# The order of phase one and of the first step of a graph attention layer, and two adjacency loads moved ahead of the first gathers

## The chip, the cores and the metric

The kernel runs on one core of a Trainium2 chip, all in fp32. The time is that of one execution on the device, in microseconds; lower is better. Engines are named as in the profile: PE is TensorE (PEld its weight loads), DVE VectorE, ACT ScalarE, POOL GpSimd, SP SyncE. SP, ACT and POOL also issue transfers; every transfer of the core runs on the same 16 DMA engines.

## The reference, cut to what matters

One graph attention layer over 4096 nodes with 256 features and 8 heads of 32. The adjacency is a 4096 x 4096 int32 matrix with few ones, dense in the first rows.

```python
mask = adj + eye(n)
q, k, v = (h @ Wq.T + bq), (h @ Wk.T + bk), (h @ Wv.T + bv)     # each as (n, 8, 32)
scores = einsum('nhd,mhd->hnm', q, k) / sqrt(32)
scores = where(mask == 0, -1e9, scores)
ctx = einsum('hnm,mhd->nhd', softmax(scores), v).reshape(n, 256)
h1 = layer_norm(h + ctx @ Wo.T + bo)
ff = relu(h1 @ W1.T + b1) @ W2.T + b2
out = layer_norm(h1 + ff)
```

## The kernel before

Rows are worked on in 32 tiles of 128. The kernel never builds the score matrix. It searches each row of the adjacency for its ones (`find_dve`, a search instruction on DVE of 4.43 us for 4104 columns), gathers the keys and values of the neighbours found from a table in memory, and scores those alone.

Phase one fills the tables. PE projects keys and values of two tiles at a time, 16 pairs, in `project_kv(i)`; each pair is 16 matmul instructions. ACT copies a pair from PSUM (`take_kv`), POOL adds the key bias (`bias_k`), and the rows go to `kv_table` in memory (`store_kv` on ACT for the last two pairs, groups of four tiles on POOL before that). Pairs of query tiles go the same way: `project_q` on PE, `take_q` on ACT, `store_q` on POOL, into `q_table`. Of the 16 query pairs, `Q_BEFORE` are projected ahead of the steps and the others in gaps of steps 0 and 1, listed by `q_pairs(step, gap)`; pair 0 is projected in the middle of phase one. `take_q(i)` waits until the store of pair i-4 has landed, since there are four staging buffers. Meanwhile DVE searches the first adjacencies, tile 0 (`TILE0`, the dense rows, in 14 pieces) among them.

A chunk of four transposed input tiles (`xT_all[c]`) serves two pairs. SP issues the chunks and the adjacencies on one queue: two halves of chunk 0, adjacency 0, chunks 1 and 2, adjacency 1, chunk 3, the adjacency of tile 0, chunks 4 to 7, adjacencies 2 and 3, weights. Adjacency s goes into buffer s % 2, once adjacency s-2 has been searched (`load_adj`).

Then come the steps `STEPS`, two tiles each at first (b0, b1_, b2, ...). For each step: `load_own` on SP loads the tiles' own rows; POOL issues gathers of 128 rows, two aligned ones (`gather_aligned`), two edge ones (`gather_edges`) and two of queries (`gather_queries`); DVE multiplies and sums the edge scores (`edge_scores_dve`) and the own scores (`own_scores_dve`); PE spreads the edge scores over rows (`ell_pe`), and prepares the next step's lists (`starts_pe`, ACT's `distance_act`, DVE's `rt_dve`, `lists_pe`, `cols_dve`, then the gathers); DVE takes the maximum, ACT the exponential, DVE the sums; DVE searches the first adjacency of the step after next; PE hands the maxima to the edges (`tr_pe`); DVE weights the values and searches the second adjacency; PE sums the values (`sum_pe`). From step 2 on, the dense work of a group of four tiles (output projection `post_pe_attn`, feed-forward `post_pe_ff`, `post_pe_out`) fills the gaps in PE's order. The program of each engine is in order, so the place of a call in these lists is its priority. The work of tile 0 is spread over later steps.

The lines of SP ahead of the steps are

```python
            load_own(sp, STEPS[0])
            sp.wait_ge(got_edges[STEPS[0].par], 2 * STEPS[0].U * 16)
            load_adj(sp, 4)
            load_adj(sp, 5)
```

and `tables_ready(eng, q)` (lines 976 to 985) is what a gather or an own load waits for: all stores of keys and values, and the store of the step's own query pair.

Of the kernel before, what the change touches and what calls it, by code (L numbers as in the profile page):

```python
# [5 lines left out]
ALU = mybir.AluOpType  # L6
# [128 lines left out]
def build(nc, xT, adj, wqkvT, bq, bk, bqkv, woT, w1T, w2T, cols, g2, be2, out):  # L135
    with ExitStack() as ctx:
# [88 lines left out]

        bias_q_cols = scores0[:, 0:D].rearrange("p (k n) -> p k n", k=KC)
# [53 lines left out]
        s_const = sem("s_const")  # L280

# [81 lines left out]
        def job(g, first_tile, at, bank, signals):  # L363
# [31 lines left out]
        (s_gw, s_gx, s_gkt_ps, s_gkt, s_gadj, s_gmask, s_gdiag, s_gxq, s_gqt_ps, s_gqt, s_gscores, s_gmasked, s_gmax, s_gnm,  # L395
         s_gprobs, s_gpt_ps, s_gpt, s_gpv, s_grl, s_gctx, s_gv, s_gctxT_ps, s_gctxT) = [sem(n) for n in (
            "s_gw s_gx s_gkt_ps s_gkt s_gadj s_gmask s_gdiag s_gxq s_gqt_ps s_gqt s_gscores s_gmasked s_gmax s_gnm "
            "s_gprobs s_gpt_ps s_gpt s_gpv s_grl s_gctx s_gv s_gctxT_ps s_gctxT").split()]

        CONSTS = 25  # L400
        WEIGHT_DMAS = 5
# [396 lines left out]
        def lists_pe(pe, q):  # L798
            pe.wait_ge(rt_ready, q.p + 1)
            pe.wait_ge(distance, 2 * q.p + 2)  # L800
# [186 lines left out]
        def gather_aligned(pool, q):  # L987
# [6 lines left out]
            tables_ready(pool, q)  # L994
# [11 lines left out]
        def gather_edges(pool, q, us=None):  # L1006
            pool.wait_ge(cols_ready, q.p + 1)
            tables_ready(pool, q)
# [6 lines left out]
        def gather_queries(pool, q):  # L1015
            pool.wait_ge(row_ready, q.b + 1)
            for u in range(q.U):
# [4 lines left out]
        def load_own(sp, q):  # L1022
            tables_ready(sp, q)
# [291 lines left out]
        def general_dve(dve):  # L1315
            with dve.Fori(0, TILES) as t:
# [5 lines left out]
                for h in range(HEADS):  # L1322
                    n = t * HEADS + h
                    dve.wait_ge(s_gscores, n + 1)
                    nc.vector.tensor_tensor(gS, flat(ps[:]), gmask, ALU.add).then_inc(s_gmasked, 1)
                    dve.wait_ge(s_gmasked, n + 1)
                    nc.vector.tensor_reduce(gstat[:, 0:1], gS, AX_X, ALU.max).then_inc(s_gmax, 1)
                    dve.wait_ge(s_gmax, n + 1)
# [75 lines left out]
        def _(sp):  # L1404
# [68 lines left out]
        def _(pool):  # L1473
# [59 lines left out]
            for q in STEPS:  # L1533
# [53 lines left out]
        def _(act):  # L1587
# [29 lines left out]
            for i in range(PAIRS):  # L1617
                take_kv(i)
# [335 lines left out]
```

## Time and profile before

| what | value |
|---|---|
| time, median of 3 runs | 555.47 us (554.21 to 555.52) |
| span of the profiled execution | 554.5 us, from its first to its last instruction; no time of its own beside the span is given for it |
| PE busy | 483.4 us, 87% of the span |
| DVE busy | 425.2 us, 77% |
| POOL busy | 262.3 us, 47% |
| ACT busy | 214.5 us, 39% |
| moved by DMA | 140.94 MB, 254 GB/s on average |
| mean granted TensorE clock | 0.937 |

Shares of busy time are averages over stages with different limits. Phase one ends near 70 us, step 0 begins on DVE at 86.6 us, step 1 at 108.5 us, step 2 at 127.8 us, and the feed-forward work begins at 148.5 us. In the rows below, the first number is the start and the second the duration, in us; in square brackets stands how long the engine sat idle before the row, and what it was released by.

### The profile page before, as it was taken

How to read it: one execution, taken by the hardware profiler on the slowest of the kernel's cores; microseconds unless marked ns; L12 is line 12 of the kernel's file. 1: busy time of each engine (PE TensorE's matmuls, PEld its weight loads, DVE VectorE, ACT ScalarE, POOL GpSimd, SP SyncE). 2: the span in 40 equal slices, each digit the busy share in tenths (PEclk: the TensorE clock that was granted, in tenths of full speed). 3: DMA queues.
4: the chain of work that ended last, by engine and by line, in shares of the span. 5: the costliest groups of instructions: out<-in, count | busy, mean ns of one | idle time of the engine just before them, and what ended most of it. 6: DMA issues, size and time to landing. Idle time of an engine off the chain costs nothing.

```text
span 554.5 us, 7282 instructions
## 1 busy us (share of the span) xinstructions
PE 483.4 (87%) x2274; PEld 376.7 (68%) x2274; DVE 425.2 (77%) x978; ACT 214.5 (39%) x526; POOL 262.3 (47%) x381
## 2 busy tenths in 40 slices
PE   5999999757699899799989989979878888789994
PEld 4888888655458757675875776668435767458883
DVE  0648696998979999999999987869988898550103
ACT  1244343324362463345336255423443143532430
POOL 6444347363633556745754553515625555305133
PEclk9999989999699999989989999978788799799998
DMA  7999868999999798998898785344765842401011
GB/s 278 418 417 418 318 214 330 400 409 420 398 329 351 266 366 261 366 348 287 323 348 318 247 292 187 138 165 148 262 222 163 302 143 58 134 1 39 0 39 42
DMA packets 39771, 140.94 MB, mean 254 GB/s; under 512 B 4904, under 2 KB 16552, under 8 KB 35632
## 3 DMA queue, kind: packets, MB, share of 16 engines
q1 hardware_dynamic: 24608, 95.03, 45.3%
q0 software_dynamic: 13328, 43.55, 22.7%
q10 hardware_dynamic: 1792, 1.85, 1.0%
q8 instruction: 20, 0.33, 0.2%
q14 instruction: 23, 0.19, 0.1%
HBM read 123.61 MB, written 16.80 MB: 253 GB/s over the span
## 4 chain that ended last, share of the span: by engine, by line
PE 51%; DVE 19%; DMA 10%; issue 8%; ACT 6%; POOL 5%; SPq 0%; POOLq 0%; ACTq 0%; DVEq 0%
PE ps L1086 15%; PE ps L1099 12%; PE ps L1719 10%; DVE found L504 6%; DMA xT_all<-in_xT 4%; PE ps L843 2%; PE ps L1066 2%; DMA work<-q_table,row_of 2%; POOL slots L1011 2%; DMA adj_buf<-in_adj 2%; PE ps L846 1%; ACT xT_all L1143 1%; PE ps L1076 1%; DMA early<-in_wqkvT 1%; PE ps L1054 1%
## 5 line engine op out<-in xcount | busy, mean ns | idle before, releaser
L504 DVE FIND_INDEX8 found<-ones,adj_buf 128x8 uint32<-128x4105 int32 (+5 forms) x40 | 138.7, 3467 | 0.0
L1086 PE MATMUL ps<-xT_all,w 128*128 128x512 f32 (+1 forms) x288 | 125.7, 585 | 0.3 <-ACT xT_all L1116 0.2
L1099 PE MATMUL ps<-w,xT_all 128*128 128x256 f32 x512 | 122.7, 395 | 2.9 <-ACT xT_all L1133 1.6
L1099 PEld LDWEIGHTS ps<-w,xT_all 128*128 128x128 f32 x512 | 99.2, 199 | 17.7 <-ACT xT_all L1133 2.7
L1086 PEld LDWEIGHTS ps<-xT_all,w 128*128 128x128 f32 x288 | 56.0, 203 | 47.6 <-issue 44.1
L1011 POOL DMA_INDIRECT slots<-kv_table,col_of x54 | 55.9, 1035 | 48.3 <-DVE col_of L587 36.4
L1133 ACT ACTIVATE xT_all<-ps,col_table 128x512 f32<-128x512 f32 (+1 forms) x72 | 45.8, 642 | 57.1 <-PE ps L1086 52.3
L1719 PE MATMUL ps<-early,xT_all 128*128 128x256 f32 x256 | 60.2, 398 | 6.1 <-DMA early<-in_wqkvT 6.1
L1719 PEld LDWEIGHTS ps<-early,xT_all 128*128 128x128 f32 x256 | 50.7, 200 | 14.2 <-DMA xT_all<-in_xT 4.7
L1153 DVE BATCH_NORM_STATS2 stats<-ps 128x6 f32<-128x256 f32 x62 | 22.1, 418 | 36.5 <-PE ps L1054 36.5
L954 ACT ACTIVATE xT_all<-ps,col_table 128x256 f32<-128x256 f32 (+1 forms) x38 | 14.5, 432 | 84.5 <-PE ps L846 84.5
L1003 POOL DMA_INDIRECT slots<-kv_table,found x32 | 33.9, 1060 | 27.8 <-PE ps L846 10.7
L1018 POOL DMA_INDIRECT work<-q_table,row_of x40 | 39.7, 992 | 11.1 <-issue 11.0
L1192 POOL TENSOR_TENSOR rstd<-mv,eps_col 128x4 f32<-128x4 f32 (+1 forms) x17 | 6.0, 355 | 76.8 <-DVE mv L1159 76.4
L843 PE MATMUL ps<-work,slots 128*128 128x128 f32 x160 | 29.2, 293 | 13.6 <-DVE slots L708 12.8
L1066 PE MATMUL ps<-wo,xT_all 128*128 128x256 f32 x128 | 35.9, 405 | 3.7 <-issue 2.5
L1735 PE MATMUL ps<-early,xT_all 128*128 128x256 f32 x128 | 36.4, 410 | 1.0 <-ACT slots L1601 1.0
L1517 POOL TENSOR_TENSOR slots<-slots,early 128x512 f32<-128x512 f32 x16 | 20.2, 1265 | 33.7 <-ACT slots L1601 33.7
L843 PEld LDWEIGHTS ps<-work,slots 128*128 128x128 f32 x160 | 24.4, 203 | 16.5 <-DVE slots L708 15.0
L1601 ACT COPY slots<-ps 128x1024 f32<-128x1024 f32 x16 | 16.2, 1013 | 41.6 <-PE ps L1719 41.6
L1003 POOL DMA_INDIRECT slots<-kv_table,aligned_idx x16 | 16.6, 1040 | 27.9 <-PE ps L846 19.9
L1201 POOL TENSOR_TENSOR early<-early,row_g 128x1024 f32<-128x1024 f32 (+1 forms) x8 | 17.8, 2227 | 25.0 <-DVE slots L708 10.4
(180 smaller groups left out, 821.7 us busy)
## 6 DMA issues: line engine op xcount, KB each, us to landing
adj_buf<-in_adj SPq DMA_DIRECT2D x31, 2048.0 KB
xT_all<-in_xT SPq DMA_DIRECT2D x14, 512.0 KB, 24.5
kv_table<-slots POOLq DMA_DIRECT2D x7, 1024.0 KB, 11.2
slots<-kv_table SPq DMA_DIRECT2D x12, 512.0 KB
q_table<-slots POOLq DMA_DIRECT2D x16, 256.0 KB
out_dram<-early SPq DMA_DIRECT2D x7, 512.0 KB
q_own<-q_table SPq DMA_DIRECT2D x12, 256.0 KB
slots<-in_adj SPq DMA_DIRECT2D x1, 2048.0 KB, 23.0
```

The lines of the kernel that those rows point to most:

```text
L504: last = nc.vector.max_index(dst, ones8[:], part)
L843: nc.tensor.matmul(to, edge_slots(q)[:, c, feats], onehot[q.par][:, c, :], start=(u == 0), stop=False)
L1003: nc.gpsimd.indirect_dma_start(to, None, kv_dram, bass.IndirectOffsetOnAxis(ap=idx, axis=0)).then_inc(got_aligned[q.par], 16)
L1011: nc.gpsimd.indirect_dma_start(edge_slots(q)[:, u, :], None, kv_dram, bass.IndirectOffsetOnAxis(ap=col_of[q.par][:, u:u + 1], axis=0)).the ...
L1018: nc.gpsimd.indirect_dma_start(q_edge[q.par][:, u, :], None, q_dram[q.no // 2], bass.IndirectOffsetOnAxis(ap=row_of[q.par][:, u:u + 1], ax ...
L1066: nc.tensor.matmul(to, q["ctxT"][:, k, j * P:(j + 1) * P], wo[:, k, :], start=(k == 0), stop=False)
L1086: last = nc.tensor.matmul(ps[:, q["bank"] + f % 2, 0:q["g"] * P], w1[:, k, f * P:(f + 1) * P], q["h1T"][:, k, :], start=(k == 0), stop=(k ...
L1099: nc.tensor.matmul(to, q["ffT"][:, f, j * P:(j + 1) * P], w2[:, f, :], start=(f == 0), stop=False)
L1133: nc.scalar.activation(q["ffT"][:, f, :], ps[:, q["bank"] + f % 2, 0:q["g"] * P], ACT.Relu, bias=bias_1[:, f:f + 1]).then_inc(q["ff"], 1)
L1153: last = nc.vector.bn_stats(q["stats"][k][:, j, :], tile_out(q, q["bank"] + 2 * k, j))
L1719: last = nc.tensor.matmul(ps[:, kv_bank(i, part), j * D:(j + 1) * D], xT_all[:, c, k, r * P:(r + 1) * P], wqkv[:, k, (1 + part) * D:(2 + p ...
L1735: nc.tensor.matmul(to, xT_all[:, c, k, r * P:(r + 1) * P], wqkv[:, k, 0:D], start=(k == 0), stop=False)
```

## The change

The change reorders phase one and the first step and touches no arithmetic.

- PE runs two matmuls on a constant tile (`warm`, 512 columns of ones that DVE writes first) before its first data. The first pair is projected by `first_kv`: keys of both tiles, then values of both tiles, where it was keys and values of one tile and then of the other.
- Query pair 0 is projected behind the last key and value pair. `Q_BEFORE` falls from 6 to 4, and pairs 4 and 5 move to gap 1 of step 0, pair 6 from gap 0 to gap 2, with their copies and stores.
- ACT stores pair 14 ahead of copying pair 15, and pair 15 at once; then it takes query pair 0; then tile 0's distances, then those of step 1 (which were in step 0).
- DVE searches adjacency 2 before it waits for tile 0's starts, and searches piece 12 of tile 0 before `rt_dve(b0)`. Tile 0's `rt_dve` comes after both searches of step 1's adjacencies. Tile 0's `cols_dve` and `onehot0_dve` move from ahead of step 0 to inside it, behind the edge scores. In step 0 the own scores come before the edge scores.
- Gathers of keys wait for the key tables alone, and only the gathers of queries and the own loads wait for the query tables.
- SP loads adjacency 4 ahead of the own rows of step 0 and adjacency 5 behind them, each when its buffer is free.
- A semaphore is saved in the fallback path, which these inputs do not take.

```diff
-        Q_BEFORE = 6
+        Q_BEFORE = 4
         def q_pairs(i, gap):
             if i == 0:
-                return ((6,), (), (7, 8), (9, 10), (11,), ())[gap]
+                return ((), (4, 5), (6, 7, 8), (9, 10), (11,), ())[gap]
...
-        def tables_ready(eng, q):
+        def keys_ready(eng):
             for i in range(STAGES):
                 eng.wait_ge(s_kv_out[i], (GROUPS // STAGES if i < STAGES - 1 else GROUPS // STAGES - 1) * 16)
-                if q.first:
-                    eng.wait_ge(s_q_out[i], PAIRS // STAGES * 16)
-            eng.wait_ge(s_kv_last, 2 * 16)
+            eng.wait_ge(s_kv_last, 2 * 16)
+
+        def queries_ready(eng, q):
+            if q.first:
+                for i in range(STAGES):
+                    eng.wait_ge(s_q_out[i], PAIRS // STAGES * 16)
             pair = (q.no + q.T - 1) // 2
             eng.wait_ge(s_q_out[pair % STAGES], (pair // STAGES + 1) * 16)
...
+            load_adj(sp, 4)
             load_own(sp, STEPS[0])
-            sp.wait_ge(got_edges[STEPS[0].par], 2 * STEPS[0].U * 16)
-            load_adj(sp, 4)
             load_adj(sp, 5)
...
+                for p in q_pairs(i, 1):
+                    store_q(p)
                 if soon:
                     gather_edges(pool, soon)
...
             for i in range(PAIRS):
+                if i == PAIRS - 1:
+                    store_kv(PAIRS - 2)
                 take_kv(i)
...
-                if i == 13:
-                    take_q(0)
+            store_kv(PAIRS - 1)
+            take_q(0)
             distance_act(act, TILE0)
-            store_kv(PAIRS - 2)
-            store_kv(PAIRS - 1)
             mask_act(act, TILE0)
+            distance_act(act, STEPS[1])
             for i in range(1, Q_BEFORE):
                 take_q(i)
...
-                if i + 1 < NB:
+                if 0 < i < NB - 1:
                     distance_act(act, STEPS[i + 1])
...
+            pe.wait_ge(warm_ready, 1)
+            for _ in range(WARM):
+                nc.tensor.matmul(ps[:, ELL, :], warm[:, 0:P], warm, start=True, stop=True)
+            first_kv()
+            for i in range(1, PAIRS):
                 project_kv(i)
...
-                if i == 13:
-                    project_q(0)
             starts_pe(pe, TILE0)
-            for i in range(1, 4):
-                project_q(i)
-            lists_pe(pe, TILE0)
-            for i in range(4, Q_BEFORE):
+            for i in range(Q_BEFORE):
                 project_q(i)
             starts_pe(pe, b1_)
+            lists_pe(pe, TILE0)
...
+            for us in ((13,), (12,)):
+                find_dve(dve, TILE0, 0, us)
+            rt_dve(dve, b0)
...
+            find_dve(dve, b1_, 0)
             starts0_dve(dve)
-            find_dve(dve, b1_, 0)
-            rt_dve(dve, TILE0)
             find_dve(dve, b1_, 1)
-            cols_dve(dve, TILE0)
-            onehot0_dve(dve)
             listed_dve(dve, b1_)
             spill_dve(dve, b1_)
+            rt_dve(dve, TILE0)
             for q in STEPS:
...
-                edge_scores_dve(dve, q)
-                own_scores_dve(dve, q)
+                if i == 0:
+                    own_scores_dve(dve, q)
+                    edge_scores_dve(dve, q)
+                    cols_dve(dve, TILE0)
+                    onehot0_dve(dve)
+                else:
+                    edge_scores_dve(dve, q)
+                    own_scores_dve(dve, q)
```

## Rows read from the trace of the kernel before

**Rows 1.** Busy us (and instructions) of each engine, granted clock, DMA share, GB/s, by stretch

```profile
70.00:80.00 10.00, 9.80 (x62) 8.69 (x60) 9.57 (x17) 5.62 (x18) 3.94 (x5) 0.94 0.65 219
...
90.00:100.00 10.00, 9.26 (x57) 8.04 (x56) 6.90 (x16) 3.79 (x10) 7.75 (x9) 1.00 0.99 416
...
150.00:175.00 25.00, 24.57 (x99) 16.09 (x98) 21.39 (x40) 10.40 (x26) 8.84 (x8) 0.99 0.94 340
```

**Rows 2.** The chain that ended last, two of its pieces: start us, us, what

```profile
70.85 5.22 DMA q_table<-slots
...
109.50 20.59 DMA xT_all<-in_xT
```

**Rows 3.** Timeline of POOL: first gather, two stores of queries

```profile
77.04 1.06 POOL L1003 DMA_INDIRECT slots<-kv_table,found  x1 [5.45 <-DMA q_table<-slots]
...
91.96 0.77 POOL L1508 DMA_DIRECT2D q_table<-slots  x1
...
97.74 1.54 POOL L1508 DMA_DIRECT2D q_table<-slots  x2
```

**Rows 4.** Timeline of DVE, 37 to 136 us

```profile
37.01 0.48 DVE L566 TENSOR_SCALAR work<-work,spill 128x128 f32<-128x128 f32 x2 [4.47 <-ACT idx_all L907]
...
68.66 0.17 DVE L559 SCALAR_TENSOR_TENSOR mids<-ps,spill 128x14 f32<-128x14 f32 x1 [3.57 <-PE ps L796]
...
80.84 0.16 DVE L575 TENSOR_SCALAR row_of<-ps 128x14 uint32<-128x14 f32 x1
...
82.05 2.88 DVE L594 TENSOR_SCALAR work<-row_mid,ps 128x128 f32<-128x128 f32 x14
...
86.58 0.69 DVE L603 TENSOR_TENSOR work<-work,slots 128x512 f32<-128x512 f32 x1 [1.09 <-DMA work<-q_table,row_of]
...
88.22 1.22 DVE L618 TENSOR_TENSOR slots<-slots,q_own 128x1024 f32<-128x1024 f32 x1
...
96.23 0.09 DVE L504 MATCH_VALUE_LOAD found<-ones,adj_buf 128x8 int32 x1 [2.90 <-DMA adj_buf<-in_adj]
...
108.50 0.68 DVE L603 TENSOR_TENSOR work<-work,slots 128x512 f32<-128x512 f32 x1
...
135.47 0.16 DVE L578 TENSOR_SCALAR row_at<-ps 128x2 f32<-128x2 f32 x1 [1.52 <-PE ps L805]
```

**Rows 5.** Busy PE and PEld, granted clock, DMA share, GB/s: key and value matmuls alone

```profile
13.00:14.00 1.00, 1.00 (x4) 0.80 (x3) 1.00 0.93 327
14.00:15.00 1.00, 1.00 (x7) 0.87 (x6) 1.00 1.09 362
```

**Rows 6.** Timeline of PE, 59 to 83 us

```profile
59.26 1.03 PE L1735 MATMUL ps<-early,xT_all 128*128 128x256 f32 x4
...
61.43 7.07 PE L1719 MATMUL ps<-early,xT_all 128*128 128x256 f32 x32
...
76.57 4.13 PE L805 MATMUL ps<-first_idx,work 128*128 128x18 f32 x28 [0.20 <-DVE work L566]
80.54 2.05 PE L1735 MATMUL ps<-early,xT_all 128*128 128x256 f32 x4
```

**Rows 7.** Load of input chunk 1 (issue at 2.8 us), with time to landing

```profile
L1407 SPq DMA_DIRECT2D xT_all<-in_xT x1: 1267/1267/1267, 2.8 to 2.8; - x1
...
DMA to landing us min/median/max: 13.4/13.4/13.4
```

**Rows 8.** Timeline of ACT

```profile
17.35 1.01 ACT L1601 COPY slots<-ps 128x1024 f32<-128x1024 f32 x1 [2.67 <-PE ps L1719]
...
68.54 1.01 ACT L1601 COPY slots<-ps 128x1024 f32<-128x1024 f32 x1 [2.44 <-PE ps L1719]
...
104.97 0.59 ACT L1607 COPY slots<-ps 128x512 f32<-128x512 f32 x1 [3.43 <-DMA q_table<-slots]
```

**Rows 9.** Stores of the last two key pairs by ACT: time to landing

```profile
DMA to landing us min/median/max: 2.9/3.4/3.9
```

**Rows 10.** Busy PE, granted clock, DMA share, GB/s after tile 0's lists

```profile
83.00:86.00 3.00, 3.00 (x11) 0.56 0.54 186
```

More of the change, by code:

```diff
@@ L799, in lists_pe @@
             pe.wait_ge(rt_ready, q.p + 1)
-            pe.wait_ge(distance, 2 * q.p + 2)
+            pe.wait_ge(distance, 2 * (STEPS[1].p if q.first else q.p) + 2)
             wait(pe, cols_ready, q.p)
@@ L1022, in load_own @@
         def load_own(sp, q):
-            tables_ready(sp, q)
+            keys_ready(sp)
+            queries_ready(sp, q)
             wait(sp, acc_ps, q.before)
@@ L1710, in project_kv @@
                     c, r = (2 * i + j) // GROUP, (2 * i + j) % GROUP
-                    if i == 0 and j == 0:
-                        pe.wait_ge(s_first_xT, 16)
                     if r == (2 if c == 0 else 0):
@@ L1715, in project_kv @@
                     for part in range(2):
-                        if i == 0 and j == 0:
-                            pe.wait_ge(s_wqkv[1 + part], 16)
                         for k in range(KC):
@@ L1720, in project_kv, with first_kv @@
                                                     wqkv[:, k, (1 + part) * D:(2 + part) * D], start=(k == 0), stop=(k == KC - 1))
+                last.then_inc(s_kv_ps, 1)
+            def first_kv():
+                order = [(j, part) for part in range(2) for j in range(2)]
+                for j, part in order:
+                    if (j, part) == (0, 0):
+                        pe.wait_ge(s_first_xT, 16)
+                    if j == 0:
+                        pe.wait_ge(s_wqkv[1 + part], 16)
+                    for k in range(KC):
+                        last = nc.tensor.matmul(ps[:, kv_bank(0, part), j * D:(j + 1) * D], xT_all[:, 0, k, j * P:(j + 1) * P],
+                                                wqkv[:, k, (1 + part) * D:(2 + part) * D], start=(k == 0), stop=(k == KC - 1))
                 last.then_inc(s_kv_ps, 1)
@@ L1741, in _ @@
             b0, b1_ = STEPS[0], STEPS[1]
-            for i in range(PAIRS):
+            pe.wait_ge(warm_ready, 1)
[3 more added lines that the diff above has]
+            for i in range(1, PAIRS):
                 project_kv(i)
@@ L1828, in _ @@
             b0, b1_ = STEPS[0], STEPS[1]
-            pieces0 = ((13,), (12,), (11,), (10,), (9,), (8, 7), (6, 5), (4, 3), (2, 1, 0))
-            for i in range(PAIRS):
-                if i == 1:
-                    dve.wait_ge(s_const, CONSTS)
-                    find_dve(dve, b0, 0)
-                if i == 3:
-                    find_dve(dve, b0, 1)
-                    listed_dve(dve, b0)
-                    spill_dve(dve, b0)
-                if i == 6:
-                    rt_dve(dve, b0)
-                if 5 <= i <= 13 and pieces0[i - 5]:
-                    find_dve(dve, TILE0, 0, pieces0[i - 5])
-                if i == 10:
-                    cols_dve(dve, b0)
-                if i == 13:
-                    listed_dve(dve, TILE0)
-                    spill_dve(dve, TILE0)
+            nc.vector.memset(warm, 1.0).then_inc(warm_ready, 1)
+            dve.wait_ge(s_const, CONSTS)
+            find_dve(dve, b0, 0)
+            find_dve(dve, b0, 1)
+            listed_dve(dve, b0)
+            spill_dve(dve, b0)
+            for us in ((13,), (12,)):
+                find_dve(dve, TILE0, 0, us)
+            rt_dve(dve, b0)
+            for us in ((11,), (10,), (9,), (8,)):
+                find_dve(dve, TILE0, 0, us)
+            cols_dve(dve, b0)
+            for us in ((7, 6), (5, 4), (3, 2), (1, 0)):
+                find_dve(dve, TILE0, 0, us)
+            listed_dve(dve, TILE0)
+            spill_dve(dve, TILE0)
+            find_dve(dve, b1_, 0)
             starts0_dve(dve)
-            find_dve(dve, b1_, 0)
-            rt_dve(dve, TILE0)
             find_dve(dve, b1_, 1)
-            cols_dve(dve, TILE0)
-            onehot0_dve(dve)
             listed_dve(dve, b1_)
             spill_dve(dve, b1_)
+            rt_dve(dve, TILE0)
             for q in STEPS:
```

18 lines of the change are left out of this document (11 added, 7 removed).

## Prediction

> **What bounds the kernel now.** I read the windows by stage first, then the chain of waits up to 150 us, then the timelines of DVE, PE, ACT and POOL. From 150 us on PE is busy 24.57 of 25 us [rows 1]: the dense work runs without a gap, so what the change can win is the time until that work starts, and all of it is then handed on to the end. Ahead of it there are three stages. Until 68.5 us the key and value matmuls follow one another. From there to 86.6 us nothing heavy is the limit: the chain goes through a store of queries of 5.22 us [rows 2], the first gather at 77.04 us [rows 3], and the landing of the last gather, for which DVE starts step 0 at 86.58 us [rows 4]. From 86.58 us DVE sets the pace: step 0 lasts until 108.50 us [rows 4], 21.92 us, with one large hole, 2.90 us of waiting for adjacency 4, which was held back behind the gathers; 19.0 us of it are work. The DMA engines are 0.65 busy from 70 to 80 us and 0.99 from 90 to 100 us [rows 1], so work moved from the second stretch to the first takes free capacity.
>
> I make the sum on the start of step 0's edge scores (86.58), the start of step 1 (108.50) and the start of dense work.
>
> **Phase one.** The first four matmul instructions wait for their weights twice, because keys and values of one tile come first. The new order has eight instructions of work with the first weights. Four instructions touch the us from 13 to 14, and seven the us after it [rows 5]: there the clock went from its low level, 1.2 GHz, to the high one, 2.4 GHz. At the high one an instruction takes 7.07/32 = 0.22 us [rows 6], so 0.43 at the low one. The warming matmuls and the new order would together finish chunk 0, 32 instructions, some 3 us earlier, were the clock high from 9 us on. But chunk 1 is issued at 2.8 us and lands 13.4 us later, at 16.2 us [rows 7], and PE finished pair 1 just before 17.35 us, when ACT copied it [rows 8]. So only about 17.2 - 16.2 = 1.0 us can be taken; with eight instructions done at 8.2 us, 24 more fit before 16.2 us even if the clock stayed low until 13.9 us. I price the warming at next to nothing and both edits at 1.0 us. Bounds: 0 if chunk 1 lands later, 1.1.
>
> Pair 0 of the queries leaves phase one: two tiles of 1.03 us and two small transposes each, from 59.26 to 61.43 us, 2.17 us [rows 6]. The copy of pair 15, at 68.54 us [rows 8], then starts at 68.54 - 1.0 - 2.2 = 65.4 us.
>
> **To the first gathers.** The bias of pair 15 is ready 2.4 us after that, 67.75 us, and ACT stores it; the last two such stores landed in 2.9 and 3.9 us [rows 9]. Keys are ready at 71.6 us. Now adjacency 4 is on the engines too, from about 66 us: DVE's hole of 3.57 us before tile 0's starts is filled by the search of adjacency 2, and most of the hole of 4.47 us at 37 us by piece 12 [rows 4], so that search ends near 66 us. A store beside a full load may take twice as long. I take 5.2 us for it, keys at 73 us, and the first gather 0.9 us later at about 74 us instead of 77.04 [rows 3]. The store of query pair 0 starts at 68.8 us and takes 5.22 us [rows 2], or some 7 beside the load: it is ready by 76 us, before the fifth gather at 79 us, so it is hidden now. From the first gather to DVE's start it was 86.58 - 77.04 = 9.54 us [rows 3, 4]. With a little for adjacency 5, which runs beside the last gathers, step 0 starts at 83.9 us, 2.7 us earlier. Bounds: 82 us (unhindered) and 86.5 us (each landing twice as long).
>
> These six gathers move 1.3 MB, in 7.4 us of issuing; at half of the 416 GB/s of a full stretch [rows 1] that takes 6.3 us, so sharing alone does not hold them up. The Trainium skill (DMA: Bandwidth & Descriptors, Queues, rings and completion order) says that each DMA engine alternates between the queues that have work, packet by packet; by that rule the gathers keep half of the rate, and the sum would stay near 83.9 us, where a strict queue behind two adjacencies would give the upper bound. It speaks against an early load all the same, since the gathers have the whole rate today.
>
> **Step 0.** The work is 19.0 us. The own scores, two instructions of 1.22 us [rows 4], leave it, because own rows and aligned gathers land first: -2.4. Tile 0's columns and one-hot rows come in, from 80.84 to 82.05 and 2.88 us more [rows 4]: +4.0. The hole of 2.90 us before the search of adjacency 4 goes, as that load has then been there for 20 us. That would be 20.6 us. But PE's order turns against it. Pairs 4 and 5, 2 x 2.17 = 4.3 us, now stand between `ell_pe` and `lists_pe` of step 1, and pairs 6 to 8, 6.5 us, ahead of `tr_pe`, where 7 and 8 were. PE finishes tile 0's lists (28 instructions, 4.13 us [rows 6]) near 80 us and then has nothing for some 5 us. At the same place the clock fell to half: a tile of queries at 80.54 us took 2.05 us instead of 1.03 [rows 6], and the clock was 0.56 from 83 to 86 us [rows 10], 1.2 GHz for most of it. PE had worked for 5 us, to about 85.6, before the clock was back [rows 6, 10], and for 6 us at the start of the kernel, from 8.2 to 14 us [rows 5]. With 5 us at half speed, PE loses 2.5 us: it resumes 1.7 us after the start of step 0, when the edge scores are made, and the lists are done at 1.7 + 0.4 + 4.3 + 2.5 + 0.4 = 9.3 us, while DVE wants them at 1.7 + 4.0 (tile 0) + 1.3 (`rt_dve`, masks, maxima) = 7.0 us. Stall: 2.3 us. Then come 6.5 us of pairs 6 to 8 and `tr_pe`, done at 16.1 us; DVE, after columns, sums and a search (5.8 us), is there at 15.1 us. Stall: 1.0 us. Step 0 is 20.6 + 3.3 = 23.9 us, 2.0 us longer than before. Bounds of the stalls: 0.5 (clock not low) to 6 us (low for twice as long). The Trainium skill (TensorE: Matmul & The Clock Gate, What's actually happening) states that the throttled clock is the default and activity releases it; the rows at 80.5 us agree, and by it the idle stretch before `ell_pe` would surely be paid.
>
> Step 1 starts at 83.9 + 23.9 = 107.8 us, 0.7 us earlier.
>
> **After step 0.** Two adjacencies, 4.2 MB or 10 us of the full rate [rows 1], have left the crowded stretch. The input of the first dense job took 20.59 us from 109.50 us to landing [rows 2] behind that backlog, and PE's output projection and step 3's lists followed; DVE stood idle 1.52 us for these lists [rows 4]. A shorter queue gives back most of it: 1.3 us (0 to 1.8). The rest of the order, the copies, masks and distances of step 1 that moved on ACT, lies beside DVE's work; the fallback's semaphore costs nothing, as that path is not run.
>
> **Sum.** -2.7 + 2.0 - 1.3 = -2.0 us, on a span of 554.5 us. The median of the runs is 0.9 us above that span, and the profiled execution has no other time; I put the change on the median: 555.47 - 2.0 = 553.5 us.
>
> **Rivals.**
> 1. PE is in time (20%). If the clock stays high or the pairs start at once, the two stalls shrink to 0.5 us or less and the gathers are unhindered: -3.9 for the start of step 0, -0.8 for step 0 itself, -1.8 behind it, together -6.5 us, 549.0 us. For it: DVE, not PE, has set this stage. Against it: the idle stretch before `ell_pe`.
> 2. The gathers pay for the adjacencies (17%): last gather at 86.5 us instead of 83.9, nothing won ahead of step 0, the rest of the sum as it stands: +2.6 on the forecast, 556.1 us, no change that a measurement could tell. For it: both loads run beside the last stores and gathers. Against it: 0.65 busy engines [rows 1].
> 3. Slower: query stores land late (18%). `take_q(10)` stood 3.43 us for a store [rows 8] that was issued at 91.96 us and landed at 104.97 [rows 3, 8], 13.0 us. The stores of pairs 6 and 7 now come behind all gathers of step 1, near 100 us (before: 91.96 and 97.74 [rows 3]), and ACT cannot do step 2's distances until both have landed. DVE wants them 4 us into step 1, behind its edge and own scores, at 111.8 us; with pair 7's store at 100.4 us and 1.8 us for ACT's copy and distances, each us of landing above 9.6 is a stall. At 13 us it costs 3.4 us (556.9); the kernel is slower than before from 11.6 us on, and measurably from 13.3. Against it: 4.2 MB are off these engines by then.
>
> **Numbers.** Forecast 45%, with its own range 551 to 555 us. A difference below 0.3%, 1.7 us, is about what a measurement of this kernel cannot tell from no change. The forecast case lies in the faster band in two of three (0.30) and in the equal one otherwise (0.15); rival 1 is faster (0.20), rival 2 mostly equal (0.13, slower 0.04), rival 3 equal in a quarter (0.04, slower 0.14). That is 0.50, 0.32 and 0.18. The range of 548.8 to 557.4 us reaches to rivals 1 and 3 and leaves out their far ends.
>
> **What would show it.** Right: pair 2's matmuls start at 16.2 us; no DVE hole before adjacency 4; the first gather near 74 us; DVE stalls for PE's lists of step 1 and for `tr_pe` in step 0, the clock low there; the first dense input lands in well under 20 us. Wrong: the first gather at 77 us or later, a stall of `rt_dve` on ACT in step 1, or dense work that starts earlier without an earlier end, because later steps wait for something I have not seen.

## The result: 567.9 us, slower by about 2%, and the profile after

The changed kernel took 567.87 us (median of 4 runs, 563.83 to 569.52) where the kernel before took 555.5 us on the same chip (4 runs, 554.21 to 559.98), a ratio of 1.0194 with a 95% interval of 1.0137 to 1.0251. A second measurement of the same kernel gave 568.01 us (6 runs) against 556.23 us (22 runs), 1.0177 (1.0143 to 1.0212). Slower is clear in both; on which side of 2% it lies is not. The forecast was 553.5 us, and neither it nor a rival reached this. All ratios are of fast runs, so they leave out the slowest one or two runs of experiments 3, 7, 9, 10 and 11 (those over 1.5% above the same kernel's fastest) and none of the kernel before, while the medians are of all runs.

The profiled execution has a span of 562.1 us and a time of its own of 563.83 us, the shortest of the four. Single executions of one kernel differ by 3 to 6 us either way here, so no single span is compared below: the profile of experiment 1, for one, is of its slowest execution. The places of the stages are steadier, and each comes from one execution all the same. On the page, busy times and bytes (140.94 MB) are as before, so the work is the same and the time is waiting:

```profile
span 562.1 us, 7278 instructions
...
PE 485.1 (86%) x2278; PEld 378.6 (67%) x2278; DVE 426.1 (76%) x979; ACT 214.2 (38%) x526; POOL 265.9 (47%) x381
```

The windows by stage, same columns as [rows 1]:

```profile
70.00:80.00 10.00, 8.56 (x54) 7.62 (x52) 6.66 (x19) 8.24 (x27) 0.73 (x1) 0.96 0.72 268
80.00:90.00 10.00, 2.72 (x13) 2.61 (x13) 0.00 (x0) 0.00 (x0) 8.08 (x9) 0.50 0.95 331
90.00:100.00 10.00, 4.04 (x13) 3.46 (x14) 8.03 (x24) 0.00 (x0) 1.99 (x2) 0.52 0.84 301
```

From 80 to 90 us DVE and ACT do nothing at all and PE 2.72 us of work, while the DMA engines are 0.95 busy: the core waits for transfers. The chain that ended last says for which:

```profile
67.37 1.02 ACT slots L1607
68.46 1.28 POOL slots L1521
...
69.76 9.50 DMA kv_table<-slots
...
79.41 0.81 issue
...
80.65 0.94 issue
81.59 10.11 DMA slots<-kv_table,found
...
91.80 1.24 DVE slots L621
```

The last key store took 9.50 us to land, where the two of before took 2.9 and 3.9 [rows 9], and the second gather 10.11 us. SP's timeline shows what ran beside them: adjacency 4 was issued at 68.76 us, ahead of that store, and landed 9.3 us later, adjacency 5 at 80.36 us, ahead of the second gather, and landed 10.5 us later.

```profile
68.76 0.33 SPq L1041 DMA_DIRECT2D adj_buf<-in_adj  x1
79.41 0.38 SPq L1033 DMA_DIRECT2D slots<-kv_table  x1
79.84 0.46 SPq L1034 DMA_DIRECT2D q_own<-q_table  x1
80.36 0.46 SPq L1041 DMA_DIRECT2D adj_buf<-in_adj  x1
```

On DVE, the rows that answer to [rows 4]:

```profile
91.80 1.22 DVE L621 TENSOR_TENSOR slots<-slots,q_own 128x1024 f32<-128x1024 f32 x1 [14.07 <-DMA slots<-kv_table,found]
...
94.19 0.68 DVE L606 TENSOR_TENSOR work<-work,slots 128x512 f32<-128x512 f32 x1
...
103.17 0.16 DVE L581 TENSOR_SCALAR row_at<-ps 128x2 f32<-128x2 f32 x1 [1.91 <-PE ps L808]
...
104.52 4.43 DVE L507 FIND_INDEX8 found<-ones,adj_buf 128x8 uint32<-128x4105 int32 x1
110.13 0.17 DVE L680 TENSOR_TENSOR p_edge<-s_edge,ps 128x16 f32<-128x16 f32 x1 [1.17 <-PE ps L828]
...
117.98 0.68 DVE L606 TENSOR_TENSOR work<-work,slots 128x512 f32<-128x512 f32 x1
...
137.95 0.69 DVE L606 TENSOR_TENSOR work<-work,slots 128x512 f32<-128x512 f32 x1 [0.47 <-DMA work<-q_table,row_of]
```

Edge scores of step 0 start at 94.19 us (before 86.58), step 1 at 117.98 (108.50), step 2 at 137.95, and the feed-forward's first product at 158.90 (148.48): 10.4 us late; the ratio of 1.0194 is 10.8 us. The search of adjacency 4 at 104.52 us has no hole before it.

### The profile page after: what moved, and what is told of

Read it like the earlier page. It is cut to its first block, busy times and chain, and to the rows that moved or that the text cites. A ratio compares the mean times of both kernels' runs of the same rounds, so it can differ in the third digit from the quotient of the medians.

```text
span 562.1 us, 7278 instructions
## 1 busy us (share of the span) xinstructions
PE 485.1 (86%) x2278; PEld 378.6 (67%) x2278; DVE 426.1 (76%) x979; ACT 214.2 (38%) x526; POOL 265.9 (47%) x381
## 2 busy tenths in 40 slices
DMA packets 39771, 140.94 MB, mean 251 GB/s; under 512 B 4904, under 2 KB 16552, under 8 KB 35632
## 4 chain that ended last, share of the span: by engine, by line
PE 39%; DVE 32%; DMA 9%; issue 9%; ACT 5%; POOL 4%; SPq 0%; POOLq 0%; DVEq 0%; ACTq 0%
DVE found L507 10%; PE ps L1092 10%; PE ps L1722 9%; PE ps L1105 8%; PE ps L1072 2%; DMA xT_all<-in_xT 2%; DVE stats L1159 2%; PE ps L846 2%; DVE slots L689 2%; DVE slots L621 2%; DMA q_table<-slots 2%; DMA slots<-kv_table,found 2%; DMA kv_table<-slots 2%; DMA work<-q_table,row_of 1%; POOL slots L1015 1%
## 5 line engine op out<-in xcount | busy, mean ns | idle before, releaser
L1092 PE MATMUL ps<-xT_all,w 128*128 128x512 f32 (+1 forms) x288 | 123.0, 575 | 0.3 <-ACT xT_all L1122 0.2
L1105 PE MATMUL ps<-w,xT_all 128*128 128x256 f32 x512 | 120.7, 390 | 2.9 <-ACT xT_all L1139 2.9
L1105 PEld LDWEIGHTS ps<-w,xT_all 128*128 128x128 f32 x512 | 97.7, 196 | 17.2 <-ACT xT_all L1139 4.4
L1015 POOL DMA_INDIRECT slots<-kv_table,col_of x54 | 58.6, 1086 | 46.0 <-DVE col_of L590 34.1
L1722 PE MATMUL ps<-early,xT_all 128*128 128x256 f32 x240 | 54.4, 389 | 2.7 <-DMA xT_all<-in_xT 2.7
L1722 PEld LDWEIGHTS ps<-early,xT_all 128*128 128x128 f32 x240 | 46.5, 195 | 9.6 <-DMA xT_all<-in_xT 3.1
L1751 PE MATMUL ps<-early,xT_all 128*128 128x256 f32 x128 | 37.6, 421 | 0.0
L621 DVE TENSOR_TENSOR slots<-slots,q_own 128x1024 f32<-128x1024 f32 (+2 forms) x19 | 24.0, 1264 | 14.1 <-DMA slots<-kv_table,found 14.1
L1607 ACT COPY slots<-ps 128x1024 f32<-128x1024 f32 x16 | 16.2, 1013 | 42.6 <-PE ps L1722 38.7
## 6 DMA issues: line engine op xcount, KB each, us to landing
adj_buf<-in_adj SPq DMA_DIRECT2D x31, 2048.0 KB, 10.5
```

Source lines behind the costliest of these rows:

```text
L621: nc.vector.tensor_tensor(keys, keys, q_own[q.par][:, 0:q.T, :].unsqueeze(2).to_broadcast([P, q.T, q.own, D]), ALU.mult).then_inc(own_scor ...
L1015: nc.gpsimd.indirect_dma_start(edge_slots(q)[:, u, :], None, kv_dram, bass.IndirectOffsetOnAxis(ap=col_of[q.par][:, u:u + 1], axis=0)).the ...
L1092: last = nc.tensor.matmul(ps[:, q["bank"] + f % 2, 0:q["g"] * P], w1[:, k, f * P:(f + 1) * P], q["h1T"][:, k, :], start=(k == 0), stop=(k ...
L1105: nc.tensor.matmul(to, q["ffT"][:, f, j * P:(j + 1) * P], w2[:, f, :], start=(f == 0), stop=False)
L1722: last = nc.tensor.matmul(ps[:, kv_bank(i, part), j * D:(j + 1) * D], xT_all[:, c, k, r * P:(r + 1) * P], wqkv[:, k, (1 + part) * D:(2 + p ...
L1751: nc.tensor.matmul(to, xT_all[:, c, k, r * P:(r + 1) * P], wqkv[:, k, 0:D], start=(k == 0), stop=False)
```

## The experiments

All were run in groups on one chip with the kernel before beside them: its medians were 557.41 us (31 runs) for the first four, 554.48 us (25 runs) for the next four, and 556.23 us (22 runs) for the last four. Compare each by its ratio. "Step 0" below is the start of its edge scores, "dense" the first product of the feed-forward, both in us from one profiled execution each.

| kernel | median us (runs) | ratio to before, 95% interval | step 0 | dense |
|---|---|---|---|---|
| kernel before | | 1 | 86.58 | 148.48 |
| changed kernel | 567.87 (4) | 1.0194, 1.0137 to 1.0251 | 94.19 | 158.90 |
| 1 adjacency 5 late | 563.45 (10) | 1.0086, 1.0054 to 1.0117 | 89.68 | 155.14 |
| 2 both late | 557.64 (10) | 1.0004, 0.9975 to 1.0033 | 83.99 | 148.28 |
| 3 before, both early | 558.87 (10) | 1.0018, 0.9978 to 1.0057 | 91.85 | 151.39 |
| 4 adjacency 4 behind own rows | 561.7 (10) | 1.0064, 1.0028 to 1.01 | 88.02 | 152.34 |
| 5 short rows | 559.92 (4) | 1.0102, 1.002 to 1.0184 | 88.22 | 153.36 |
| 6 chunk 1 first | 554.49 (10) | 1.0003, 0.9966 to 1.0039 | 82.10 | 149.38 |
| 7 pairs back | 553.38 (10) | 0.9964, 0.9929 to 0.9999 | 82.38 | 146.82 |
| 8 no warming | 555.93 (10) | 1.0012, 0.9978 to 1.0046 | 82.33 | 148.13 |
| 9 pairs back, chunk 1 first | 553.29 (11) | 0.9919, 0.9886 to 0.9951 | 81.82 | 146.34 |
| 10 pair 6 in gap 1 | 555.52 (12) | 0.9956, 0.9921 to 0.999 | 82.61 | 147.72 |
| 11 both of 9 and 10 | 554.33 (6) | 0.989, 0.9848 to 0.9932 | 81.94 | 146.59 |
| 12 changed kernel again | 568.01 (6) | 1.0177, 1.0143 to 1.0212 | 93.92 | 160.21 |

The places have a noise of their own. In the profiles of the changed kernel (both) and of experiments 2 and 4 PE's clock dipped early in phase one (see 6 and 8), and the last copy of keys started at 67.2 to 67.4 us; in those of 1, 5, 7, 8 and 10 it did not, and the copy started at 65.5 to 65.8 us. Up to 1.9 us of a difference between the two groups is therefore not the edit's.

### 1 to 4: which load, beside what

Experiment 1 holds back adjacency 5 alone, 2 both, 4 lets adjacency 4 go behind the own rows; 3 puts both loads early in the kernel before, the rest of it untouched.

```diff
 1          load_adj(sp, 4)
            load_own(sp, STEPS[0])
+           sp.wait_ge(got_edges[STEPS[0].par], 2 * STEPS[0].U * 16)
            load_adj(sp, 5)
 2          load_own(sp, STEPS[0]); the wait; load_adj(sp, 4); load_adj(sp, 5)
 3 (before) load_adj(sp, 4); load_own(sp, STEPS[0]); load_adj(sp, 5)
 4          load_own(sp, STEPS[0]); load_adj(sp, 4); the wait; load_adj(sp, 5)
```

> The changed kernel with adjacency 5 held back behind the first gathers again; adjacency 4 stays early. Theory A (the two early loads share the DMA engines with the last key store and with the first gathers, and each small transfer lands only when the adjacency beside it has landed): the key store still lands near 79 us, but the gathers, from 80.2 us, land as in the kernel before, 9.5 us later; step 0's scores start near 89.5 us instead of 94.2, and the time is some 4 to 5 us under that of the changed kernel, above the kernel before by 3 to 7 us. Rival B (the new order of step 0, the later query pairs and stores cost the time, and the loads are innocent): start of step 0 and time within 2 us of the changed kernel.

> The changed kernel with adjacencies 4 and 5 both behind the first gathers, as in the kernel before; the whole new order of phase one and step 0 stays. Theory A: the last key store lands in under 4 us (near 73.7 us), the first gather starts near 75 us, step 0 starts near 84.5 us and step 1 near 108 us; time 554 to 556 us, within 0.3% of the kernel before. Rival B: the time stays 5 us or more above the kernel before.

> The kernel before with the loads alone changed: adjacency 4 ahead of the own rows, adjacency 5 behind them, no wait for the first gathers. Theory A: adjacency 4 starts at 73.3 us, beside the store of query pair 0 (70.9 us), and adjacency 5 at 81 us beside the last gathers, so step 0 starts 3 to 6 us later than 86.6 us; the hole before adjacency 4 (2.9 us) goes; time 1 to 4 us above the kernel before. Rival B: step 0 starts at 86.6 us, the hole goes, and the time is up to 3 us below the kernel before.

> The changed kernel with adjacency 4 behind the own rows of step 0 (so behind the last key store and the first query store) and adjacency 5 behind the gathers. Theory A: the key store lands as without a load (near 73.7 us), adjacency 4 starts near 76.5 us in the middle of the gathers, and the gathers land late, near 87 to 89 us; time 2 to 4 us above that of the version with both loads late. Rival B: the same time as with both late.

With both loads late (2), the last two key stores land in 3.5 and 2.8 us, and the first gather no longer waits for them but for DVE's search of the last adjacency ahead of it:

```profile
73.45 1.07 POOL L1007 DMA_INDIRECT slots<-kv_table,found  x1 [1.67 <-DVE found L507]
```

With adjacency 4 early and 5 late (1) it does, as long as in the changed kernel:

```profile
80.18 1.06 POOL L1007 DMA_INDIRECT slots<-kv_table,found  x1 [10.23 <-DMA kv_table<-slots]
```

Stores, gathers and times of 1 and 2 came out as expected under theory A, so rival B, the innocent loads, is out. The start of step 0 goes from 83.99 us (2) to 89.68 us (1) and to 94.19 us in the changed kernel. So in this order adjacency 4 early costs 5.7 us, through the last store's landing, and adjacency 5 early 4.5 us, through the gathers: together 10.2 us. This sum compares two profiles that both have the dip, and is the firm figure. The split goes over experiment 1, which had none: against experiment 8, with both loads late and no dip either (82.33 us), adjacency 4 costs 7.4 us. Adjacency 5's share can be read within the stage: from first gather to step 0 it took 13.97 us in the changed kernel and 9.50 us in 1, with the first gather at 80.2 us in both. The ratios stand in the same order, 1.0004, 1.0086 and 1.0194. Experiment 4 moves adjacency 4 off the stores and onto the gathers (issued at 74.45 us, where 76.5 was expected): stores as in 2 and the first gather at 73.29 us, but the own scores wait 7.86 us for a gather, and step 0 starts at 88.02 us. Whichever of the two runs beside the load pays.

The hole that the early loads were there to close is gone without them. In experiment 2, with the loads issued at 83.98 us, DVE goes straight on from the probabilities to the search:

```profile
95.28 0.21 DVE L668 TENSOR_TENSOR own_p<-scores,top_rec 128x32 f32<-128x32 f32 x1
95.39 0.08 DVE L507 MATCH_VALUE_LOAD found<-ones,adj_buf 128x8 int32 x1
95.46 4.43 DVE L507 FIND_INDEX8 found<-ones,adj_buf 128x8 uint32<-128x4105 int32 x1
```

The tile-0 work and PE's stalls, which the new order puts ahead of that search in step 0, cover the load. So in the new order the early loads cost 10.2 us at the start of step 0 and win nothing. In the old order (3) they do win the hole of 2.90 us, and they cost less: SP issues adjacency 4 at 72.50 us, behind the last stores, which land in 2.9 to 4.0 us. The gathers pay alone, step 0 starts 5.3 us late (in an execution whose last copy came 0.8 us sooner than before's), the dense work 2.9 us late, and the time differs by less than can be measured. One rise in price comes from phase one itself: the new order searches adjacency 2 earlier (until 68.74 us), so its buffer is free earlier, and adjacency 4 leaves 1.0 us ahead of the last key store instead of behind it.

### 5: is it the length of the adjacency's rows?

The changed kernel, with adjacencies 4 and 5 loaded as eight pieces of 512 columns, 2 KB a row.

```diff
+        PARTS = 8
...
-            sp.dma_start(adj_buf[s % 2][:, 1:1 + N], adj[t * P:(t + 1) * P, :]).then_inc(adj_loaded[s % 2], 16)
+            n = PARTS if s in (4, 5) else 1
+            for c in range(n):
+                cols = slice(c * N // n, (c + 1) * N // n)
+                sp.dma_start(adj_buf[s % 2][:, 1 + cols.start:1 + cols.stop], adj[t * P:(t + 1) * P, cols]).then_inc(adj_loaded[s % 2], 16)
```

> The changed kernel, both loads as early as it has them, but adjacencies 4 and 5 loaded as eight pieces of 512 columns each, so that one row of a piece is 2 KB, as large as a row of the key store, where the whole adjacency has rows of 16 KB. Theory A1 (the DMA engines take turns between queues by packet, and the adjacency's packets are eight times as large, so a small transfer gets a small share and lands only when the adjacency has landed): the last key store lands in 5 to 6 us instead of 9.5, the gathers in 4 to 6 us instead of 10, step 0 starts near 87 us, the time is 4 to 8 us under that of the changed kernel. Rival A2 (whatever is issued later waits for all bytes ahead of it): store and gathers land as late as in the changed kernel, and the time is the same as its.

The queues of the changed kernel while the last key store is under way, 69 to 79 us (packets, MB, share of the 16 engines' time; q1 is SP's queue, with the adjacency, q10 ACT's, with the store):

```profile
q1 hardware_dynamic: 144, 2.10, 63.0%
q10 hardware_dynamic: 277, 0.53, 13.7%
```

The same with short rows, 68 to 76 us:

```profile
q1 hardware_dynamic: 842, 1.55, 64.8%
q10 hardware_dynamic: 315, 0.60, 19.3%
```

An adjacency's packets average 2.10 MB / 144 = 14.6 KB, a store's 0.53 MB / 277 = 1.9 KB. If the engines take turns by packets, the store has 1.9 / 16.5 = 12% of the bytes as long as both queues have work, and most of it moves when the adjacency is through: that landed at 68.76 + 9.3 = 78.1 us, the store at 79.3 us. The same view over shorter stretches shows whether they do:

| kernel and stretch, us | q1: packets, MB | the other queue: packets, MB |
|---|---|---|
| changed kernel, 71 to 73 | 45, 0.74 | store (q10): none |
| changed kernel, 74 to 76 | 33, 0.54 | store (q10): 35, 0.07 |
| changed kernel, 76 to 79 | 19, 0.05 | store (q10): 229, 0.44 |
| changed kernel, 84 to 89 | 101, 1.61 | gathers (q0): 82, 0.29 |
| adjacency 4 behind own rows, 79 to 84 | 97, 1.59 | gathers (q0): 79, 0.27 |
| short rows, 71 to 74 | 326, 0.60 | store (q10): 265, 0.51 |
| short rows, 83 to 88 | 503, 0.92 | gathers (q0): 311, 0.99 |

Beside long rows the queues move about one packet each, and the short rows get 11 to 15% of the bytes; beside short rows they get about half. A strict order of issue, in which an earlier transfer moves whole before a later one, does not fit: the gathers issued behind adjacency 5 moved 82 packets to its 101. For the store it does look like one at the start: the store was issued at 69.76 us and had no packet before 73 us, while with the loads late (2, issued at 69.74 us) it moved 67 packets from 70 to 71 us already. That delay of about 3 us is there with short rows too (issued at 68.24 us, moving in earnest from 71 us), and its cause is open. So the store pays twice: it starts late, and then it waits for the adjacency packet by packet; 0.44 of its 0.52 MB moved from 76 us on, when the adjacency was all but through.

With short rows the store landed in 6.3 us instead of 9.5, the first gather came at 75.55 us instead of 80.22, and step 0 6.0 us sooner. Of these 6.0 us, 1.5 are the earlier last copy (no dip in this profile), 3.2 the store, and 1.3 the gathers: from the first of them to step 0 it still took 12.67 us, after 13.97, so the expected "4 to 6 us instead of 10" for the gathers did not come. The edit also changes more than the length of the rows: SP took from 67.61 to 72.89 us to issue the eight pieces, and two of them, 0.5 MB, were ahead of the store, where the changed kernel has the whole 2.1 MB ahead. How much of the 3.2 us is that, and how much the turns, was not told apart.

The gathers' bytes show the same. The changed kernel from 81 to 91 us, six gathers under way beside adjacency 5 (q0 is POOL's queue):

```profile
q1 hardware_dynamic: 648, 2.80, 74.5%
q0 software_dynamic: 186, 0.65, 25.3%
```

With both loads late, 74 to 84 us:

```profile
q0 software_dynamic: 489, 1.57, 46.8%
q1 hardware_dynamic: 544, 0.79, 24.8%
```

Gathers and query stores moved 0.65 MB in 10 us beside the adjacency and 1.57 MB without it. With short rows it was 1.16 MB from 76 to 86 us.

The Trainium skill (DMA: Bandwidth & Descriptors, Queues, rings and completion order) has each DMA engine alternate between queues packet by packet. The counts above agree for the packets of the profile, 35 to 33 and 82 to 101, once the store has begun; whether the page means the packets that the profile counts, no run here shows. What the prediction made of it, half of the rate, would follow only for packets of one size.

### 6 and 8: phase one

```diff
 6 (both late)
-            load_adj(sp, 0)
             load_xT(1)
+            load_adj(sp, 0)
 8 (both late)
-        WARM = 2
+        WARM = 0
```

> The version with both loads late, with one more edit: input chunk 1 is issued ahead of adjacency 0. Theory: the start of pair 2 at 16.3 us is the landing of chunk 1, behind which the warming and the new order of the first pair lose what they win, and the wait of 2.65 us also lowers the clock for a while. With chunk 1 in time the last copy of keys and values starts near 63.5 us instead of 67.3, the gathers and step 0 start 3 to 4 us earlier (step 0 near 80.5 us), and the time is 2 to 4 us under both kernels. Rival: DVE's searches (tile 0 and step 1's first) end at the same time as before and hold the start of step 0, so the time moves by less than 1.5 us.

> The version with both loads late, without the two warming matmuls. Theory: the start of pair 2 is set by the landing of chunk 1 at 16.3 us with and without them, so nothing is lost; the last copy starts within 0.7 us of 67.3 us and the time stays within 0.2%. Rival: the warming is what brings pair 2 to 16.3 us, and without it the copy starts 1 us or more later.

In the changed kernel PE waits at 16.36 us for chunk 1, as forecast:

```profile
10.07 3.62 PE L1722 MATMUL ps<-early,xT_all 128*128 128x256 f32 x16
16.36 13.82 PE L1722 MATMUL ps<-early,xT_all 128*128 128x256 f32 x55 [2.67 <-DMA xT_all<-in_xT]
```

The window behind that wait has a granted clock of 0.71:

```profile
16.00:20.00 4.00, 3.64 (x12) 3.01 (x13) 3.58 (x1) 0.00 (x0) 0.92 (x2) 0.71 1.05 440
```

Without the warming matmuls (8) PE comes later and waits 1.47 us, but goes on at the same time, and 64 instructions take 14.08 us at the high clock:

```profile
11.10 3.62 PE L1723 MATMUL ps<-early,xT_all 128*128 128x256 f32 x16
16.19 14.08 PE L1723 MATMUL ps<-early,xT_all 128*128 128x256 f32 x64 [1.47 <-DMA xT_all<-in_xT]
```

The last copy of keys came at 65.5 us there. It came at 67.2 to 67.4 us in the two profiles of the changed kernel and in experiments 2 and 4, where the clock dipped, and at 65.5 to 65.8 us in experiments 1, 5, 7 and 10, whose phase one is the same and where it did not. So the warming matmuls buy nothing here, since chunk 1 sets the pace either way, and the longer wait was followed by a dip in four of eight profiles. With chunk 1 first (6) the wait is gone and the copy comes at 63.76 us, 3.6 us earlier than in experiment 2, but step 0 only 1.9 us earlier; against experiment 8, which had no dip, it is 1.75 us for the copy and 0.2 us for step 0. The last stores now run beside other transfers of phase one and land in 4.6 to 5.9 us, and the first gather waits 3.56 us for them. Its time is no better than before's, where 2 to 4 us less were expected.

### 7, 9, 10, 11: PE's order

```diff
 7 (both late)
-        Q_BEFORE = 4
+        Q_BEFORE = 6
-                return ((), (4, 5), (6, 7, 8), (9, 10), (11,), ())[gap]
+                return ((6,), (), (7, 8), (9, 10), (11,), ())[gap]
...
+            for i in range(4, Q_BEFORE):
+                project_q(i)
 9 (7, and chunk 1 ahead of adjacency 0, as in 6)
10 (7)
-                return ((6,), (), (7, 8), (9, 10), (11,), ())[gap]
+                return ((), (6,), (7, 8), (9, 10), (11,), ())[gap]
11 (9 and 10)
```

In 7, pairs 4 and 5 stand behind tile 0's lists, in the time in which PE had nothing to do.

> The version with both loads late, with query pairs 4, 5 and 6 back ahead of step 0's first matmul (pairs 4 and 5 behind tile 0's lists) and 7 and 8 ahead of tr_pe, as in the kernel before. Theory: in step 0 DVE stands 3.03 us for PE's lists and 1.17 us for tr_pe because these pairs were moved behind its first matmul and run at the low clock after an idle stretch of PE; with them back both stalls go, step 1 starts 3 to 4 us earlier, the time is 2 to 4 us under the version with both loads late. Rival: the stalls move to the first matmul of step 0, which then waits for pair 6, and the time stays within 1 us.

> Both adjacencies behind the gathers, the order of phase one with the query pairs moved back by one (the order that timed 553.38), and chunk 1 of the inputs issued ahead of adjacency 0. If the start of step 0 follows phase one's last copy, the copy comes at about 63.8 instead of 65.5 to 67.4 and step 0 starts at 81 to 82.5; since the last key stores then go beside loads that still run (landing 5 to 6 instead of 3), at most 1 us of it is left: 552 to 554. If the stores and gathers take all of it, no change from that order: 553 to 554.

> The order that timed 553.38, with query pair 6 multiplied in the first gap of step 0 instead of ahead of it. In that order VectorE waited 2.76 us in step 0 for the sum of ell from TensorE, since TensorE came from the pairs ahead of the step. If that is the reason, the wait goes under 1.5 us, step 1 starts 1 to 2 us earlier (at about 104.5) and the time is about 552. If TensorE owes the same work anyway before step 1's first product, the wait only moves to there and the time stays at 553 to 554.

> Both edits together: pair 6 in the first gap, chunk 1 ahead of adjacency 0. If the two are independent, 551 to 553; if the query stores for steps 1 and on set the feed-forward's start, no better than the better of the two alone.

In experiment 2 DVE stood 3.03 and 1.17 us for PE in step 0. In 7 both are gone and one of 2.76 us, for the edge scores that `ell_pe` spreads ("ell"), stands in their place:

```profile
91.37 0.27 DVE L649 TENSOR_TENSOR scores<-ps,mask 128x112 f32<-128x112 f32 x1 [2.76 <-PE ps L820]
```

Step 0 is 105.81 - 82.38 = 23.4 us long instead of 24.9 (24.4 in experiment 8, which has the stalls and no dip in phase one). Step 1 started 3.1 us sooner than in 2, as expected, but 1.6 us of that was the sooner start of step 0. Moving pair 6 (10) takes the wait for ell to 0.31 us, as expected, but step 1 does not come sooner: a wait of 1.62 us for the lists and one of 1.98 us for the gather at the start of step 1 come in its place, and step 1 starts at 107.37 us, 1.6 us later than in 7:

```profile
89.19 0.28 DVE L649 TENSOR_TENSOR scores<-ps,mask 128x112 f32<-128x112 f32 x1 [0.31 <-PE ps L820]
91.77 0.16 DVE L581 TENSOR_SCALAR row_at<-ps 128x2 f32<-128x2 f32 x1 [1.62 <-PE ps L808]
...
107.37 0.69 DVE L606 TENSOR_TENSOR work<-work,slots 128x512 f32<-128x512 f32 x1 [1.98 <-DMA work<-q_table,row_of]
```

Experiment 11 starts step 1 at 104.86 us, 0.8 us before 9, and then DVE waits 2.51 us for ACT's copy of an index in step 1 (9: 1.57 us); both reach step 2 at 127.1 to 127.2 us. The two runs' intervals overlap, and 11 has 6 runs between 547.96 and 558.24 us, so they are not told apart. Experiment 9 is faster than the kernel before by 0.8% (0.5 to 1.1%) by its ratio, and by 0.5% by the medians, 553.29 us against 556.23. Its interval overlaps that of 7 (0.9929 to 0.9999), so whether chunk 1 first adds anything to the order of 7 is not shown.

### 12: the changed kernel again

> The changed kernel itself again, for a tighter figure beside the others. Additive reading: adjacency 4 early costs 5.7 us and adjacency 5 early 4.5 us at the start of step 0, so 9 to 11 us above the kernel before, ratio 1.015 to 1.022, feed-forward starting about 10 us later. If the first figure was chance, under 1.012.

The ratio came out as expected, 1.0177; the medians are 11.8 us apart, a little above the 9 to 11. Its profile repeats the first: first gather at 79.91 us after 8.17 us of waiting, step 0 at 93.92 us, dense work at 160.21 us.

## Why the prediction was wrong, point by point

**The steps that failed: the last key store's landing and the gathers beside adjacency 5.** "A store beside a full load may take twice as long. I take 5.2 us for it" measured 9.50 us (9.2 in the second profile), above the bound of twice 3.9. "With a little for adjacency 5" put 9.9 us between the first gather and step 0; it measured 94.19 - 80.22 = 13.97 us. Step 0's start missed by 94.19 - 83.9 = 10.3 us: 2.0 us from the last copy (67.4 instead of 65.4), 4.3 from that landing, and 4.1 from the gathers. The argument took the engines' busy share of 0.65 [rows 1], a third idle, for room that the store could use, and half of the rate for what a gather keeps. Neither held beside a neighbour whose packets are about eight times as long. The bound of 86.5 us, "each landing twice as long", was too narrow by the same reasoning, and with it the range. That the early loads are the cause was shown by 1, 2 and 4. That the length of their packets is part of it is shown by the counts of packets (35 to 33, and 0.07 to 0.54 MB) and supported by 5, which staggered the issue as well. The store's late first packet, 3 us after its issue, is the other part, and why it comes late is open. One thing came out milder than forecast: the search of adjacency 2 ended at 68.74 us and not near 66, so adjacency 4 was under way 1.0 us ahead of the last store and not 2.

**What the loads would win.** The hole before adjacency 4 was counted as their gain (-2.90). It did go, but experiment 2 shows that it closes without them. The shorter queue later was worth nothing either: the first dense input landed in 15.7 us instead of 20.59 [rows 2], "well under 20", but it was issued at 119.97 us, and from step 1's start (9.5 us late) to the dense work (10.4 us late) the kernel lost another 0.9 us where 1.3 were to be won.

**Phase one, right but for the clock.** Chunk 1 landed at 16.3 us (forecast 16.2), and the two terms of 1.0 and 2.2 us gave 65.5 to 65.8 us for the last copy where the clock held. In the profiled execution the dip after the wait of 2.67 us took 1.6 to 1.9 us of them, a cost that was not in the sum. One reading needs a word: [rows 5] have a granted clock of 1.00 in both of their stretches, and that it rose there was read from the matmuls, four in one us and seven in the next, and not from that column.

**Step 0, right, in part by luck.** It took 117.98 - 94.19 = 23.79 us, forecast 23.9; the stalls for PE were 1.91 and 1.17 us, forecast 2.3 and 1.0, and the clock was 0.52 from 90 to 100 us, as the argument on the idle stretch wanted. PE's idle stretch was 13.23 us, though, and not the 5 us of the argument, as step 0 came late; with 4.69 us of it, in experiment 2, the first stall was 3.03 us and step 0 24.9 us long. It is these stalls that eat what phase one wins: in experiment 2, step 0 starts 2.6 us before that of the kernel before and step 1 0.4 us after. The new order alone is worth nothing that can be measured (1.0004, 0.9975 to 1.0033).

**The rivals.** The second, the gathers pay for the adjacencies, named the right place, and its price of 2.6 us was a quarter of the real one. The first was tested by experiment 7: with PE's pairs put back the order gives 0.36% (0.01 to 0.71%), 0.2% by the medians, where the rival had 6.5 us or 1.2%. The third did not decide: ACT waited 6.30 us for a store of queries that took 10.43 us to land, but DVE stood only 0.41 us for it in step 1:

```profile
119.28 0.58 ACT L1613 COPY slots<-ps 128x512 f32<-128x512 f32 x1 [6.30 <-DMA q_table<-slots]
```

The forecast of 83.9 us for step 0 fits experiment 2, 83.99, by accident: a copy 1.9 us later, a last store 2.4 us shorter, and 0.6 us more for the gathers than it assumed.

## What to carry to other kernels

A transfer in long rows beside short ones is not a neighbour with an equal share: before a large load is moved to an earlier place, list the small stores and gathers on which the next stage waits, and price each at the load's whole duration, not at twice its own (here 9.5 and 10.1 us beside loads of 9.3 and 10.5 us). An idle share of the DMA engines was room here only for what nothing on the critical path ran beside. And a load held back on purpose is worth freeing only if the search that needs it would still wait; here other edits had closed that hole. A last habit: before two profiles of one stage are compared, look whether the stages ahead of it ended alike; here a dip of the clock in four of the profiles moved what came behind it by up to 1.9 us.

## What the runs showed of the hardware that was not expected

- A store of 512 KB in 2 KB rows took 2.8 to 4.0 us with no adjacency beside it (experiments 2 to 4 and before; 4.6 to 5.9 us beside other transfers in 6), 9.2 to 11.3 us when an adjacency in rows of 16 KB was issued 0.6 to 1.0 us ahead of it (the changed kernel twice, and 1), and 6.3 us when the same adjacency went in eight pieces of 2 KB a row (5).
- Beside an adjacency in 16 KB rows, another queue moved about one packet for each of its packets, whatever their lengths (35 to 33, 82 to 101, 79 to 97), but the store's first packet came only some 3 us after its issue.
- PE's granted clock fell after a wait for chunk 1 in four of eight executions of the same phase one (0.57 to 0.71 from 16 to 20 us, against 1.00), and the waits were 2.65 to 2.67 us with the fall and 2.63 to 2.65 us without. In the four with it (changed kernel twice, 2 and 4) PE was still at its first eight key and value matmuls at 7.5 us; in the four without (1, 5, 7 and 10) they were done by 7.25 us. What links the two was not tested.
- The granted clock was 0.50 from 80 to 90 us, where PE had 2.72 us of work, and a tile of queries took 2.03 us at 96.85 us instead of 1.03. That was no second price of the late gathers: in experiment 2, with a PE idle stretch of 4.69 us instead of 13.23, the tile of queries took 2.03 us as well.
